# A softmax kernel with running adding DMAs: two semaphores for even and odd heads, and a head's loads issued at three places

## The reference

```
q, k, v = split(xn @ qkvw + qkvb)                 # 32 heads, head dim 32
scores  = einsum('bhqd,bhkd->bhqk', q, k) * 32**-0.5
probs   = softmax(scores)                          # max, exp, sum, divide
ctx     = einsum('bhqk,bhkd->bhqd', probs, v)
out     = x + ctx @ ow + ob + lora(xn)
```

## Time and profile before

| | |
|---|---|
| median of three runs | 2737.16 us |
| profiled execution, its own time | 2734.81 us |
| its span | 2732.7 us |
| TensorE busy in the span | 2588.2 us (95%) |
| GpSimd busy | 1612.5 us (59%) |
| VectorE busy | 1505.5 us (55%) |
| ScalarE busy | 1221.3 us (45%) |

### The profile page before, as it was taken

How to read it: one execution, slowest core, us unless ns; L and a number is a source line. 1 busy time by engine, 2 the same in 40 slices (tenths; PEclk the granted TensorE clock), 3 DMA queues, 4 the chain that set the end, 5 groups by cost and what they waited for, 6 DMA issues and landing times. The chain is left out here.

```text
span 2732.7 us, 34876 instructions
## 1 busy us (share of the span) xinstructions
PE 2588.2 (95%) x13032; PEld 1662.3 (61%) x13032; DVE 1505.5 (55%) x2522; ACT 1221.3 (45%) x2299; POOL 1612.5 (59%) x529
## 2 busy tenths in 40 slices
PE   7999999999799999999999999999999999979999
PEld 6888887777555555455555555545554555527887
DVE  8411111111398777777777777777776777613221
ACT  3111111110046666666666666656665666652000
POOL 0111111110048899899889989989988998972111
PEclk9999999999779999999999999999999999999999
DMA  4233333113537767766767776776686777524332
GB/s 146 85 116 117 122 122 116 69 69 100 129 75 147 152 138 143 155 141 142 162 134 143 151 151 143 142 154 140 137 165 133 144 150 152 121 57 164 107 107 96
DMA packets 168168, 351.01 MB, mean 128 GB/s; under 512 B 89632, under 2 KB 114720, under 8 KB 137376
## 3 DMA queue, kind: packets, MB, share of 16 engines
q0 software_dynamic: 22320, 162.54, 30.2%
q1 hardware_dynamic: 145712, 186.70, 24.5%
HBM read 122.44 MB, written 63.69 MB: 68 GB/s over the span
## 5 line engine op out<-in xcount | busy, mean ns | idle before, releaser
L909 DVE TENSOR_REDUCE part_max<-ps_b 128x1 f32<-128x512 f32 x2048 | 1256.2, 681 | 398.4 <-PE ps_b L788 397.8
L736 POOL TENSOR_TENSOR psum_p<-psum_p,probs 128x2048 f32<-128x2048 f32 x254 | 1200.9, 4728 | 10.5 <-ACT probs L895 0.4
L895 ACT ACTIVATE probs<-ps_b 128x512 f32<-128x512 f32 x1924 | 972.8, 622 | 355.8 <-PE ps_b L777 350.2
L777 PE MATMUL ps_b<-qp,kp 97*128 97x512 f32 x2048 | 849.5, 418 | 28.4 <-DMA qp<-neg_max 23.2
L788 PE MATMUL ps_b<-kp,qp 96*128 96x512 f32 x2048 | 836.0, 416 | 14.5 <-DMA qp<-qk_scr 14.3
L777 PEld LDWEIGHTS ps_b<-qp,kp 97*128 97x128 f32 x2048 | 388.2, 190 | 384.1 <-issue 215.5
L804 PE MATMUL ps_b<-probs,vh 128*32 128x512 f32 x3848 | 472.3, 604 | 0.0
L788 PEld LDWEIGHTS ps_b<-kp,qp 96*128 96x128 f32 x2048 | 401.3, 196 | 103.7 <-DVE part_max L909 38.5
L236 POOL TENSOR_TENSOR wlo<-wraw,whi 128x1024 fp32r<-128x1024 f32 x29 | 69.4, 2395 | 612.6 <-ACT whi L339 612.6
L265 PE MATMUL ps_a<-xhi,whi 128*128 128x512 f32 (+1 forms) x928 | 370.3, 399 | 1.1 <-DVE elo L428 0.9
L265 PE MATMUL ps_a<-xlo,whi 128*128 128x512 f32 (+1 forms) x928 | 367.2, 396 | 0.0
(11 more groups left out here) (79 smaller groups left out, 1165.2 us busy)
## 6 DMA issues: line engine op xcount, KB each, us to landing
psum_q<-probs POOLq DMA_DIRECT2D x155, 1024.0 KB, 7.8
kp<-qk_scr SPq DMA_DIRECT2D x96, 256.0 KB, 7.7
qp<-qk_scr SPq DMA_DIRECT2D x96, 256.0 KB, 8.2
qk_scr<-ehi SPq DMA_DIRECT2D x16, 1024.0 KB, 3.9
qk_scr<-elo SPq DMA_DIRECT2D x16, 1024.0 KB, 6.7
wraw<-wcat SPq DMA_DIRECT2D x29, 512.5 KB, 7.5
craw<-cz_scr SPq DMA_DIRECT2D x16, 768.0 KB, 4.9
stage<-x SPq DMA_DIRECT2D x16, 512.0 KB, 3.8
```

The lines of the kernel that those rows point to most:

```text
L736: pool.tensor_tensor(acc[:, :], first[:, :], tile(h, t)[:, :], ALU.add).then_inc(pool_done, 1)
L777: pe.matmul(ps[:, n % ST_BANKS, :], kp[s][0:PACK + 1, t * P:(t + 1) * P], qp[s][0:PACK + 1, b * NQ:(b + 1) * NQ], start=True, stop=True).t ...
L895: act.activation(tile(h, t)[:, b * NQ:(b + 1) * NQ], ps[:, n % ST_BANKS, :], ACT.Exp, scale=SCALE).then_inc(exp_done, 1)
L909: dve.tensor_reduce(part_max[hn % 2][:, tn, b:b + 1], ps[:, ring_bank(u), :], AX_X, ALU.max) \
```

## The change

`chained` becomes two semaphores, one for even and one for odd heads; each counts only its own heads' DMAs. An adding DMA still waits for the one before it in its own head, and for the last one of head h-2 (which had the same `psum_q` buffer), no longer for that of head h-1. `load(h)` is cut into three: keys stay where they were; queries come after `store_ctx(h-2)` and after a further wait, for `pv_done` at 16 h + 4 (tiles 0 to 3 of head h are multiplied with the values); the values come after `invert_sums(h-1)`, ahead of `load_negmax(h+1)`. Sizes, numbers of DMAs and arithmetic stay.

```diff
-        chained = sem("chained")
+        chained = [sem("chained0"), sem("chained1")]
...
-            return 16 * (len(CHAIN_TILES) * h + CHAIN_TILES.index(t) + 1)
+            return 16 * (len(CHAIN_TILES) * (h // 2) + CHAIN_TILES.index(t) + 1)
...
             for h in range(SLOTS):
-                load(h)
+                load_keys(h)
+                load_queries(h)
+                load_values(h)
...
                 if h >= 1:
                     sp.wait_ge(pv_done, TT * h)
                     if h + 2 < HEADS:
-                        load(h + 2)
+                        load_keys(h + 2)
                     if h >= 2:
                         store_ctx(h - 2)
+                    if h + 2 < HEADS:
+                        sp.wait_ge(pv_done, TT * h + 4)
+                        load_queries(h + 2)
                     invert_sums(h - 1)
+                    if h + 2 < HEADS:
+                        load_values(h + 2)
                 if h < LAST:
                     load_negmax(h + 1)
...
-                wait(pool, chained, chain_count(h, t) - 16)
+                wait(pool, chained[h % 2], chain_count(h, t) - 16)
                 pool.wait_ge(exp_done, 64 * h + 4 * t + 4)
                 pool.sem_inc(cleared, 1)
-                pool.dma_start(psum_q[h % 2][:, :], tile(h, t)[:, :], accum_op=ALU.add).then_inc(chained, 16)
+                pool.dma_start(psum_q[h % 2][:, :], tile(h, t)[:, :], accum_op=ALU.add) \
+                    .then_inc(chained[h % 2], 16)
...
-                pe.wait_ge(chained, chain_count(h, CHAIN_TILES[-1]))
+                pe.wait_ge(chained[h % 2], chain_count(h, CHAIN_TILES[-1]))
...
-                    act.wait_ge(chained, chain_count(hp, tp))
+                    act.wait_ge(chained[hp % 2], chain_count(hp, tp))
```

More of the change, by code:

```diff
@@ L655, in _, with load_keys, load_queries, load_values @@
         def _(sp):
-            def load(h):
-                s = h % SLOTS
-                q_row, k_row = h * HD, h * HD + D
+            def load_keys(h):
+                s, row = h % SLOTS, h * HD + D
                 for r, hl in enumerate((0, 1, 0)):
-                    sp.dma_start(kp[s][r * HD:(r + 1) * HD, :].bitcast(F32), qk_scr[hl, k_row:k_row + HD, :]) \
+                    sp.dma_start(kp[s][r * HD:(r + 1) * HD, :].bitcast(F32), qk_scr[hl, row:row + HD, :]) \
                         .then_inc(kq_loaded[s], 16)
+            def load_queries(h):
+                s, row = h % SLOTS, h * HD
                 for r, hl in enumerate((0, 0, 1)):
-                    sp.dma_start(qp[s][r * HD:(r + 1) * HD, :].bitcast(F32), qk_scr[hl, q_row:q_row + HD, :]) \
+                    sp.dma_start(qp[s][r * HD:(r + 1) * HD, :].bitcast(F32), qk_scr[hl, row:row + HD, :]) \
                         .then_inc(kq_loaded[s], 16)
-                c = h % 4 * HD
+            def load_values(h):
+                s, c = h % SLOTS, h % 4 * HD
                 sp.dma_start(vh[s][:, :, :], v_scr[h // 4].rearrange("p (t c) -> p t c", c=P)[:, :, c:c + HD]) \
```

## The result

The changed kernel takes 2617.18 us (median of four runs, 2614.72 to 2617.83) against 2736.72 us for the kernel before on the same chips: a ratio of 0.956, 95% interval 0.9545 to 0.9578. That is 119.5 us less. The profiled execution took 2617.83 us, its span is 2615.8.

The account below looks back on a forecast made before the run. The GpSimd and tile 14 DMA loop was taken as the bound. From the profiled 2734.8 us: -111.6 for 29 heads at 48.5 instead of 52.35, -3 for head 31, +20 allowance gave 2640; +2.3 gave 2642 us, range 2620 to 2712.

Parts of the forecast that it names:

- The pace was the loop GpSimd, tile 14's DMA, GpSimd: GpSimd's 40.4 us of work plus tile 14's 11.8 us landing set a head's 52.4 to 53.5 us, slowing TensorE.
- TensorE's own 48.4 us: On TensorE: its own work is some 48.4 us a head, the next bound once the loop is gone.
- The cross-check: Between the marks: 1518.1 us less 81.4 idling, less 2% lost clock (30), is 1407 us or 48.5 a head.
- The wait ahead of `sums`: TensorE's 58.2 us of idling in 24 heads, for an adding DMA, was to go whole.
- Keys, queries, values: 0: SyncE's moved loads cost TensorE 0; bounds 0 to 29 x 1 us for queries, 0 to 72 us for values.
- The stated loss of up to 2.5 us for values ahead of the row: On SyncE: values delay the maxima row 1 to 2.5 us less 3 us cover; rival 2650 to 2680 us, chance 0.08.
- The order of the maxima row and tile 12's DMA: Late in a head: the row is issued 0.3 us ahead of tile 12's adding DMA and so lands quickly.
- four heads of 29 in which the maxima row falls behind: At heads' starts: an allowance of 5.1 us each, 3.4 TensorE wait plus 1.7 lost clock, +20 us in all.
- Head 31's -3: At head 31's start, past the 29 heads: a wait of its own, with its clock, goes, -3 us.
- The last step: From the profiled execution's 2640 us to the median of the runs: 2.3 us added, giving 2642 us.
- the shared wait wasn't the pace: Rival: GpSimd's additions or the DMA engines hold 52 us a head anyway, 2732 to 2742 us; chance 0.04.
- A row behind in all heads: Rival: maxima row behind tile 12's DMA in nearly every head, 53.6 us each, 2773 or 2815 us; chance 0.12.

Follow-up runs that it names:

- the landing shortened alone: Only the three separate places for keys, queries and values, one semaphore for all heads, against the kernel before: 2630.48 us, ratio 0.9604.
- the kernel with groups of one: The changed kernel with the values' product tile by tile at every step, not two tiles at every second: 2684.78 us, ratio 0.9807 to the kernel before.
- the kernel with the row behind: The changed kernel with a SyncE wait for step 14's row maxima ahead of the maxima row's load: 2802.83 us, ratio 1.0235 to the kernel before.

## Why the prediction was off, point by point

- **The pace was the loop GpSimd, tile 14's DMA, GpSimd.** Right. With the shared count cut alone the 6.4 us of idling go and the whole gain follows; with the landing shortened alone, 107 us of it follow (40.4 + 7.3 + 0.5).
- **TensorE's own 48.4 us.** Right, and the mean was 48.34; the sum had 48.5. Here the forecast gave away 4.6 us. The cross-check that led to 48.5 took the lost clock from a mean of 0.98, rounded.
- **The wait ahead of `sums`.** Right: gone in all heads; tile 14's DMA is issued 6.8 us into a head ("some 6") and lands by 16.
- **Keys, queries, values: 0.** Right in this kernel. The queries' wait and issue hold up nothing. The stated loss of up to 2.5 us for values ahead of the row shows only where they are issued shortly before it (none here, 8.4 us ahead), and in part by another way: SyncE's long issue.
- **The order of the maxima row and tile 12's DMA.** Here is the failed step: "I allow four heads of 29 in which the maxima row falls behind: + 4 x 5.1 = +20". It was none, and two things were wrong in it. First, the lead was worked out as 0.3 us; it is 1.27. I let GpSimd run back to back from tile 4 on, by the earlier trace rows, where it had a backlog. Caught up, it waits 1.31 us for tile 7, because the sums (1.9 us of TensorE at step 6) delay the scores of steps 7 and 8. The same sums were counted in TensorE's schedule and not in GpSimd's. Second, 0.3 us was called thin, though the one row at hand said otherwise (0.21 us ahead, landed in 1.4 us); with 0.04 us, in the kernel with groups of one, the row lands in 1.8 us in the median. So even the lead as computed asked for no allowance. The mechanism of a row that falls behind was right in kind, as the kernel with the row behind shows, but a head then costs 6.2 us more (54.5 against 48.3) and not 5.1, as the clock takes 2.6 us and not 1.7. That the lead "is measured in one quick head" doesn't hold either: head 1's GpSimd wasn't yet free of the loop, and its tile 12 came 5.8 us behind the row (868.90). Its timeline in the kernel before (the view names ScalarE, but tile 3 was made by 837.4; the DMA of the tile 14 before it, issued at 832.31, landed at 843.8):

```profile
844.33 0.87 POOL L751 DMA_DIRECT2D psum_q<-probs  x1 [6.08 <-ACT probs L895]
...
874.66 0.86 POOL L751 DMA_DIRECT2D psum_q<-probs  x1
```

- **Head 31's -3.** Wrong: next to nothing is gained there (345.2 against 345.7 us), as TensorE had no wait for the row there to lose: all 19 of the earlier trace rows lie ahead of it. Only 0.8 of the 117.0 us lie outside the 29 heads. The terms together, 20 + 4.6 - 2.2 = 22.4, are what lies between the forecast for the profiled execution (2640.2) and its time. The last step, 2.3 us from the profiled execution to the median, was chance: this time the median lies 0.65 us below the profiled one.
- **The range.** With no head falling behind and 48.4 us a head the working itself gives 2734.8 - 29 x 3.95 - 3 + 2.3 = 2619.5. The lower end of 2620 left out the best case that the text had worked out, and any spread around it; the measured 2617.2 is 2.4 us below that case.

The rivals: that the shared wait wasn't the pace falls with the two semaphores alone. A row behind in all heads didn't happen, but made to happen it costs 65 us against the kernel before (forecast: +36 to +78).

## What to carry to other kernels

Look for a loop that passes through a wait on a shared counter: one semaphore for two buffers makes a DMA wait for another that it has nothing to do with, and everything else is slowed to it, so that the engine that is 95% busy looks like the bound. Two cures of one loop don't add. And when an engine is freed, recompute its schedule from the data that it then waits for, with all of the delays on that data; the order of a small urgent DMA and a large one hangs on it.

## What the runs showed that I had not expected

- Issuing an 8 KB DMA right behind the values' (256 KB in 128-byte pieces) took SyncE 1.3 us in the median and up to 3.3 us, against 0.55 us, and up to 5.05 us some 2.5 us behind the values with an adding DMA in flight. What the issue waits for, no run here shows.
- An idle TensorE of 3.6 us ahead of each head cost another 2.6 us in clock; a wait there counted for 1.7 times its length.
- The row need not be issued ahead of the adding DMA to be quick: 0.04 us ahead and 0.15 us behind it landed in 1.8 us, 0.55 us behind in 4.7 to 5.2 us.
- The adding DMA can take 11.7 us instead of 7.3 at no cost at all once everything that waits for it comes later still (the sums by 1.8 us in the head shown).
